# Graph network on one core: in the edge sorts, VectorE waits for each operation of an exchange before it issues the next

## The reference, cut to what matters

```python
edge_index = jnp.stack([src, dst])
h = jnp.maximum(_layernorm(x, axis=-1), 0.0)
x = x + _L0_gnn_ref(h, edge_index, ...)     # softmax over the edges of a node, then a small MLP
h = jnp.maximum(_layernorm(x, axis=-1), 0.0)
x = x + _L1_gnn_ref(h, ...)                 # MLP with batch norm on x[row], x[col], summed by row
h = jnp.maximum(_layernorm(x, axis=-1), 0.0)
x = x + _L2_gnn_ref(h, edge_index, edge_attr_3, ...)   # two spline convolutions, summed by dst
h = jnp.maximum(_layernorm(x, axis=-1), 0.0)
x = x + _L3_gnn_ref(h, edge_index, edge_attr_8, ...)   # three edge convolutions, summed by dst
```

## Time and profile before

| what | value |
|---|---|
| median of 3 runs | 8720.19 us (8714.68 to 8742.84) |
| profiled execution, span | 8766.9 us |
| its own time beside the span | none shown |
| VectorE busy | 3983.5 us (45%), 7722 instructions |
| GpSimd busy | 5206.6 us (59%), 5117 instructions |
| TensorE busy | 2754.5 us (31%) |
| ScalarE busy | 1560.4 us (18%) |
| phase "sort" | from the start to about 1492 us |

### The profile page before, as it was taken

One profiled execution on the slowest core, in us unless ns is written; L12 is line 12 of the kernel. 1 busy time (PEld: TensorE's weight loads), 2 busy tenths in 40 slices (PEclk: granted clock), 3 DMA queues, 4 the chain that ended last, 5 costly groups with the idle time before them and its releaser, 6 DMA issues. The chain is left out here.

```text
span 8766.9 us, 40351 instructions
## 1 busy us (share of the span) xinstructions
PE 2754.5 (31%) x8087; PEld 1661.8 (19%) x8087; DVE 3983.5 (45%) x7722; ACT 1560.4 (18%) x2650; POOL 5206.6 (59%) x5117
## 2 busy tenths in 40 slices
PE   0000000001422400025754456477433344344322
PEld 0000000001311200002321334355322222222211
DVE  7676548980244530013643567576566322222111
ACT  0000001200111200014753112122244211111100
POOL 7736741787177587772245666456477566566566
PEclk9999999995655655557877556677655555555555
DMA  2100100111322100001111122132244333233111
GB/s 50 24 19 21 24 16 6 23 36 43 116 46 44 20 18 23 22 7 30 46 46 36 41 44 49 36 54 52 48 92 92 54 56 53 45 54 51 46 43 38
DMA packets 436186, 365.20 MB, mean 42 GB/s; under 512 B 123871, under 2 KB 412164, under 8 KB 435575
## 3 DMA queue, kind: packets, MB, share of 16 engines
q0 software_dynamic: 163392, 77.79, 10.2%
q1 hardware_dynamic: 252780, 256.09, 9.3%
q10 hardware_dynamic: 19786, 28.92, 1.0%
HBM read 206.39 MB, written 158.75 MB: 42 GB/s over the span
## 5 line engine op out<-in xcount | busy, mean ns | idle before, releaser
L907 POOL DMA_INDIRECT g_ring<-tab,QB x784 | 754.1, 962 | 459.8 <-issue 232.2
L907 POOL DMA_INDIRECT c_ring<-tab,QB x784 | 776.7, 991 | 420.8 <-issue 222.0
L1584 PE MATMUL c_psU<-spline,c_hzT 97*128 97x288 f32 x1568 | 656.2, 577 | 295.6 <-DVE c_V L1539 199.5
L907 POOL DMA_INDIRECT l_ring<-in_x_dram,a_own x392 | 447.1, 1141 | 381.9 <-POOLq L102 262.8
L907 POOL DMA_INDIRECT nodes_ring<-nodes,b_own x320 | 314.6, 983 | 546.7 <-DMA x2d_lin<-nodes_ring 449.5
L907 POOL DMA_INDIRECT l_ring<-agg_tab,QA x392 | 393.5, 1004 | 342.8 <-POOLq L102 180.4
L907 POOL DMA_INDIRECT H<-xe_tab,idx_a x392 | 411.4, 1050 | 275.8 <-DVEq L777 156.7
L907 POOL DMA_INDIRECT c_ring<-nodes,b_other x392 | 386.5, 986 | 261.7 <-issue 129.0
L907 POOL DMA_INDIRECT rows_b<-b_edges,idx_b x392 | 433.4, 1106 | 151.5 <-issue 137.3
L2213 POOL DMA_INDIRECT out_dram<-out_rowr,out_idxr x392 | 385.4, 983 | 197.3 <-issue 128.1
L1584 PEld LDWEIGHTS c_psU<-spline,c_hzT 97*128 97x128 f32 x1568 | 402.2, 274 | 469.9 <-issue 266.8
(11 more groups left out here) (544 smaller groups left out, 7996.6 us busy)
## 6 DMA issues: line engine op xcount, KB each, us to landing
tab<-c_rows SPq DMA_DIRECT2D x147, 128.0 KB
nodes<-l_decay ACTq DMA_DIRECT2D x40, 322.3 KB
nodes_x<-nodes SPq DMA_DIRECT2D x50, 257.8 KB
c_din<-dst_lin SPq DMA_DIRECT2D x98, 128.0 KB
c_ring<-tab SPq DMA_DIRECT2D x98, 128.0 KB
c_ring<-tab,QB POOLq DMA_INDIRECT x784
dst_lin<-c_yd SPq DMA_DIRECT2D x98, 128.0 KB
g_din<-dst_lin SPq DMA_DIRECT2D x98, 128.0 KB
```

What stands on the lines that cost most here:

```text
L907: pool.indirect_dma_start(out=ring[:, at + j, :], out_offset=None, in_=table, in_offset=bass.IndirectOffsetOnAxis(ap=idx[:, w:w + 1], axis ...
L1584: ins = pe.matmul(self.psU[i % 2][:, t, 0:288], self.hzT[c % 2][:, (2 * i + t) * P:(2 * i + t + 1) * P], w[:, :, :].rearrange("p o j -> p ...
```

## The change

Both helpers use `link(...)`, which waits for all increments so far, where they used `link.inc(...)` and a common wait behind the group:

```diff
     def exchange(self, v, link, of, to):
         (x, y), (lo, hi) = of, to
-        link.inc(v.tensor_tensor(lo, x, y, ALU.min))
-        link.inc(v.tensor_tensor(hi, x, y, ALU.max))
-        v.wait_ge(link.sem, link.base + link.n)
+        link(v.tensor_tensor(lo, x, y, ALU.min))
+        link(v.tensor_tensor(hi, x, y, ALU.max))
 
     def exchange_with(self, v, link, of, to, wof, wto, m, d):
         (x, y), (lo, hi), (wx, wy), (wlo, whi) = of, to, wof, wto
-        link.inc(v.tensor_tensor(m, x, y, ALU.is_gt))
-        link.inc(v.tensor_tensor(d, wy, wx, ALU.subtract))
-        link.inc(v.tensor_tensor(lo, x, y, ALU.min))
-        link.inc(v.tensor_tensor(hi, x, y, ALU.max))
-        v.wait_ge(link.sem, link.base + link.n)
+        link(v.tensor_tensor(m, x, y, ALU.is_gt))
+        link(v.tensor_tensor(d, wy, wx, ALU.subtract))
+        link(v.tensor_tensor(lo, x, y, ALU.min))
+        link(v.tensor_tensor(hi, x, y, ALU.max))
         link(v.tensor_tensor(d, d, m, ALU.mult))
-        link.inc(v.tensor_tensor(wlo, wx, d, ALU.add))
-        link.inc(v.tensor_tensor(whi, wy, d, ALU.subtract))
-        v.wait_ge(link.sem, link.base + link.n)
+        link(v.tensor_tensor(wlo, wx, d, ALU.add))
+        link(v.tensor_tensor(whi, wy, d, ALU.subtract))
```

## The result

| what | before | after |
|---|---|---|
| median of 20 runs, us | 8682.1 (8650.1 to 8748.3) | 8671.46 (8538.9 to 8754.5) |
| mean of the same 20 runs, us | 8693.7 | 8648.6 |
| ratio | | 0.9883, 95% interval 0.9855 to 0.9911 |
| span of the profiled execution | 8766.9 | 8586.8 |
| start of the second gather | 699.5 | 679.4 |

The change makes the kernel faster, by 1.2% in the ratio and by 0.5% in the mean of all runs; the forecast was 25 us, 0.3%, slower. The changed kernel's times lie in two groups, nine of the 20 from 8539 to 8622 us and eleven from 8665 to 8755, and over all 20 the medians are only 0.1% apart. The ratio counts ten of the upper ones as slow runs and leaves them out, though their granted clock, 0.685 to 0.692, is no lower than the others' 0.683 to 0.688. So 1.2% is the gain in the lower group. The changed kernel's profile is of an execution of that group.

A forecast was written before the change was run, and what follows sets the result against it. VectorE was taken to set the end from 28 to 1492 us. Added waits of 12.4 + 6.0 + 1.3 + 5.6 = 25 us on the 8720 us median gave 8745 us, range 8500 to 8870.

The forecast's parts named there:

- VectorE sets the end of the phase: From 28 to 1492 us VectorE, not the gathers, sets the end, so longer exchanges move everything behind them.
- The clear price: Where VectorE hardly idles, added waits cost 0.125 us a pair and 0.50 us an exchange_with.
- The charge of 1.40 us per operation in a stall: While GpSimd gathers, each stalled VectorE operation takes 1.40 us, whether it is waited for or not.
- The added wait then costs nothing: In stalled stretches the added waits cost nought, except 8.5 us in the first sort, of which 5.6 us stays.
- the stalls go: Lower bound for the price in the stalled stretches: their idle time beside the gathers vanishes, -426 us.
- The first rival: Stalls under gathers need two operations in flight; without them 8361 us, half gone some 8550; chance 0.26 wholly or in part.
- The sign that I had set for it: Stretches under a gather with 0.03 us idle between operations would show the first rival right.
- The second and third rival: Second: each added wait costs a 0.70-us step in stalls, 8872 us, chance 0.16. Third: waits are free, 8720 us, 0.10.

The follow-up runs named there:

- the held kernels: The kernel before and the changed kernel, each with the second gather started only behind the third sort: 7343.7 and 7411.8 us.
- paced: Changed kernel, join's exchange_with back in groups, added sequencer steps behind each operation: one in the riding merge, two in the third sort; 8812.9 us, ratio 0.9965.
- slow_pair_b: Kernel before with one more VectorE sequencer step behind each exchange, minimum and maximum still going out together; 8747.6 us beside 8757.4, one run.
- late_slow: Changed kernel with a 128x256 GpSimd memset ahead of each step of both gathers from chunk 24 on; 8464.5 us, ratio 0.9725.
- pause_bare: Kernel before with one more semaphore step of GpSimd's sequencer ahead of every gather step, no memset; 7034.9 us beside 7032.4, one run.

## Why the prediction was wrong

The range, 8500 to 8870 us, held the time; the direction was wrong. By its steps:

- **VectorE sets the end of the phase: right** in sessions with stalls. Layer norm and phase end both came 95.9 us sooner, and the gathers kept their length.
- **The clear price, 0.125 us a pair and 0.50 us an `exchange_with`: right.** L266 starts 0.72 us behind L265, and the held kernels differ by 62.6 us in the sorts for 67. That their whole times differ by 68.1 is partly luck. The Trainium skill's rule in "VectorE: DVE Perf Modes", section "The DRAIN you can't avoid", that the semaphore costs nothing extra, doesn't hold for these operations.
- **The charge of 1.40 us per operation in a stall, whether waited for or not: right.** Of the kernel before, 143 operations take 200 us; of the changed one, single narrow ones stall at 1.40 each. In `paced` semaphore steps were charged on top.
- **"The added wait then costs nothing": this is the step that failed.** I priced an operation within the stalled stretches and took the stretches as given. But the same waits that add 0.12 us to a pair in clear time also decide whether the second sort is clear at all, and from 143 to 267 operations in 200 us is worth far more than the waits cost. In the two profiles `joined`, forecast some 12 us later, came 20.1 us sooner, and the stretch behind the second gather's end, forecast longer, was 72.9 us shorter. The working did have the place for it, the lower bound "the stalls go", and I took the other end because the stalled rows showed no dependence on waits. Rows from inside a stalled stretch can't show what starts one.
- **The first rival: right in its direction, wrong in its mechanism and too large.** It gave 8361 us with all stalls gone and 8550 with half. The phase lost 142 of its 478 us of VectorE's idle time. The sign that I had set for it did come, 0.03 us idle between operations under a gather: (200.00 - 191.06) / 267 from 740 to 940 us. It was no proof, for `slow_pair_b` ran its second sort clear with the pairs in flight, and single operations stall.
- **The second and third rival: wrong.** No wait cost a step of 2.1 us throughout, and L266 isn't 0.61 us behind L265.

What stays open: why 0.11 or 0.12 us in a pair decides in the second sort and not in the first; why some executions stall from the first sort's start; what sets in some 15 us into the third sort; and what makes a session one without stalls. One and the same chip number showed both, and no kernel was made to bring the stalls back. Whether the pause from the first step on beats `late_slow` where there are stalls was tried twice and not answered. The changed kernel itself was not run in a session without them.

## What to carry to other kernels

When idle time on an engine comes in equal steps beside another engine's work, price a change for where that state starts as well as for what one instruction costs inside it, and give both signs a large chance. Test from the other engine's side as well: here a 0.13-us memset before each indirect DMA of GpSimd removed more of VectorE's stalls (285 us idle to 15) than any wait or step added to VectorE did (180 us at best). And measure such a cure where nothing stalls as well: there the pauses cost 1.5%.

## What was unexpected of the hardware

- In the second sort VectorE is either clear or charged 1.40 us an operation, 143 of them in 200 us, and in the third sort operations of 0.42 us are charged the same as those of 0.69. In the stall of `paced` its sequencer's semaphore steps took 0.70 or 1.40 us each, in that of `slow_pair_b` 0.02.
- In the three kernels that tried it, a pause between GpSimd's indirect DMAs took the stall away: with 0.13 us of memset per step, none is left beside steps of 1.46 us in the mean. Plain steps take 1.25 us in the median beside a stalled VectorE, and 1.33, 1.44 or 1.45 us beside a clear one, as long as its pair.
- The same kernel takes 7020 to 7032 us in some sessions and 8682 to 8757 in others. In a faster one `pause_bare`, as fast as the kernel before, has VectorE busy for 167 of the 172 us up to 200 us (248 operations), and the rest of the program takes it 5958 us in place of 7274, so the later phases differ too, not the sorts alone.
